# Two-stage expert layer: 17 tiles sorted from the first 24 row tiles run right behind the output projection, 22 tiles after them

## The chip, the cores and the metric

One NeuronCore of a Trainium2 chip runs the whole program. The time is device microseconds of one execution, the median of three; a separate, profiled execution gives the trace. Engines are named as in the profile: PE (TensorE matmul), PEld (its weight loads), DVE (VectorE), ACT (ScalarE), POOL (GpSimd), SP (SyncE, which here only issues transfers).

## The reference

The input x has 4 sequences of 1024 rows of 512 values (4096 rows, 32 row tiles of 128). An RWKV-like layer comes first, then one expert out of eight for each row:

```python
x_prev = x shifted by one row within its sequence
xk, xv, xr = x_prev + (x - x_prev) * tmk, ... * tmv, ... * tmr
k, v, r = xk @ Wk.T + bk, xv @ Wv.T + bv, xr @ Wr.T + br
wkv = scan over time of exponentially weighted averages of v (weights from k)
x1 = layernorm(x + (sigmoid(r) * wkv) @ Wo.T + bo)
probs = softmax(x1 @ wg)                      # 8 experts
e = argmax(probs); gate = probs[e]            # one expert a row
out = layernorm(x1 + gate * (x1 @ W[e].T + b[e]))
```

All is float32. Products that need the accuracy are made as three products of a split operand (`hi` and `lo` parts of float32r: hi*hi, hi*lo, lo*hi).

## The kernel before

**First phase.** The rows are cut into 8 blocks of 512 (`BLOCKS`). `walk` runs a `step` for each block on every engine, with a written-out tail for the last block (`last`; `before` and `earlier` are the two ahead of it). In a block PE makes the projections K, V, R in four chunks of 128 channels (12 matmuls each), DVE runs the scans (`recurrence`, `running_max`, `distance`), POOL makes the `lo` halves (`mix_lo`) and two sums per chunk (`leave`), ACT the exponentials. For a chunk pair ACT gives a reciprocal (`reciprocal_guess`), which waits for DVE's `denominator`, and DVE turns it into the result (`try_guess`, `refine`, `result`, which raises `wkv_done`). The output projection (`project_out`, for the last block `out_last`) waits for `wkv_done`. DVE adds the residual (`add_rows`, `add_last`), ACT normalises (`norm`, `norm_last`), PE turns the rows (`turn_rows`, `turn_last`) and makes the router's logits (`logits`, `logits_last`) after ACT has moved the turned rows (`move_turned`, `move_last`). SP stores the rows x1 to memory.

**Routing.** On DVE, `largest` and `choose` make a one-hot matrix of the chosen expert, PE's `count` multiplies it by a triangular matrix (each row's rank within its expert), and DVE works out each row's place in the sorted list: `split_dest` (to integers and back), `place_slots` and `place_tiles` (one-hot matrices for the place within a tile and for the tile). PE multiplies them (line 609) into the list of row numbers, and DVE writes `ids`. The first 24 row tiles (`EARLY`) are counted before the last 8 (`LATE`), but the list is made once, from all 32. Each chained small operation of DVE goes through `link`, which waits for the end of the one ahead of it.

**Second phase.** 39 tiles (`SORTED` = 32 + 7) of up to 128 rows of one expert each. POOL gathers a tile's rows by `ids` with an indirect transfer, PE turns them (`turn`), ACT copies (`move_gathered`), DVE splits (`split_gathered`), PE makes 12 matmuls (`expert`), DVE adds bias and residual (`add_bias`, `add_gathered`), ACT normalises (`norm2`), POOL scatters to the output. PE turns two tiles ahead. SP loads one bias row for each tile. The experts' weights are split by ACT (`expert_hi`) and then by POOL (`expert_lo`, experts 0 to 4; DVE 5 to 7). POOL splits expert 0 before its last `leave` and the others after `wkv_done` of the last block.

The order of the work is written out by hand on each engine; engines meet only at semaphores:

```python
def link(ins):
    chain[0] += 1
    ins.then_inc(routed, 1)
    dve.wait_ge(routed, chain[0])
...
expert_lo(0)
leave(last, CH - 1)
pool.wait_ge(wkv_done, last * 2 + 2)
for e in range(1, POOL_EXPERTS):
    expert_lo(e)
```

## Time and profile before

| | us |
|---|---|
| median of 3 runs (lowest, highest) | 676.62 (675.92, 677.89) |
| the profiled execution's own time | 679.24 |
| its span in the trace | 677.3 |
| first to last tile of experts on PE | 523.64 to 664.0 |
| PE busy of the span | 591.4 (87%) |
| DVE, ACT, POOL busy | 554.9, 403.9, 307.3 |

The span is what the trace covers; 1.9 us of the profiled execution's own time lie around it. Times of rows count from the span's start. A row that gives "x4" stands for four instructions in a run, and its duration is that of the run. What stands in brackets at a row's end is the idle time of the engine ahead of it and who ended that.

### The profile page before, as it was taken

The page shows a single profiled execution, that of the slowest core. Times are in us where ns is not written, and L with a number is a line of the kernel's source. Part 1 is how long each engine was busy: PE and PEld are TensorE (multiplying, and loading weights), DVE is VectorE, ACT ScalarE, POOL GpSimd, SP SyncE. Part 2 cuts the span into 40 slices and gives each one's busy share as a digit, 9 for nine tenths or more (in the row PEclk, how much of TensorE's full clock was granted, in tenths as well). Part 3 has the DMA queues.
Part 4 walks back from the last instruction along what each step waited for, and adds up shares of the span by engine and source line. Part 5 has one row for each costly group of instructions (what it writes and reads, how often), then busy time and mean ns, then how long its engine had stood idle before and what let it go on. Part 6 is the DMA issues. An engine that isn't in the chain of part 4 may idle for free. (4 is left out here: it accounts for less than half of the span.)

```text
span 677.3 us, 8986 instructions
## 1 busy us (share of the span) xinstructions
PE 591.4 (87%) x2484; PEld 438.7 (65%) x2485; DVE 554.9 (82%) x866; ACT 403.9 (60%) x735; POOL 307.3 (45%) x230
## 2 busy tenths in 40 slices
PE   0576788999999999999999999998665999899992
PEld 0355665676778667668768767855464777676771
DVE  7948899998999999999999899678956566566661
ACT  3346475477567656756757647566331677577773
POOL 4743544443551552463444444248304356465541
PEclk9679899999999999999999999898955899899997
DMA  8030010031022013104104103392204576577650
GB/s 309 3 124 1 0 63 0 2 109 62 16 84 72 32 33 122 31 0 155 31 0 148 41 0 125 137 382 103 59 20 140 147 219 211 184 218 216 213 174 6
DMA packets 36562, 67.60 MB, mean 100 GB/s; under 512 B 8560, under 2 KB 8560, under 8 KB 36532
## 3 DMA queue, kind: packets, MB, share of 16 engines
q1 hardware_dynamic: 30292, 48.29, 21.8%
q0 software_dynamic: 6240, 18.94, 9.0%
q8 instruction: 15, 0.25, 0.2%
q14 instruction: 15, 0.12, 0.1%
HBM read 50.17 MB, written 18.88 MB: 102 GB/s over the span
## 5 line engine op out<-in xcount | busy, mean ns | idle before, releaser
L971 POOL TENSOR_TENSOR mixed<-unsplit,mixed 128x1024 fp32r<-128x1024 f32 x44 | 104.5, 2396 | 133.7 <-ACT mixed L657 133.7
L447 PE MATMUL kb<-mixed,w_kvr 128*128 128x512 f32 x384 | 97.9, 405 | 24.4 <-DVE mixed L1312 16.5
L447 PE MATMUL vb<-mixed,w_kvr 128*128 128x512 f32 x384 | 103.1, 420 | 14.9 <-DVE evn L1150 8.6
L629 PE MATMUL y_ps<-w_e_hi,xgT 128*128 x312 | 110.1, 415 | 3.2 <-issue 1.7
L447 PE MATMUL rb<-mixed,w_kvr 128*128 128x512 f32 x384 | 101.8, 415 | 5.5 <-DVE ee L1164 3.6
L447 PEld LDWEIGHTS kb<-mixed,w_kvr 128*128 128x128 f32 x384 | 73.7, 195 | 43.1 <-issue 16.2
L465 PE MATMUL y_ps<-w_o,rw 128*128 128x512 f32 x224 | 100.7, 592 | 0.0
L447 PEld LDWEIGHTS vb<-mixed,w_kvr 128*128 128x128 f32 x384 | 74.5, 198 | 36.8 <-DVE evn L1150 11.8
L447 PEld LDWEIGHTS rb<-mixed,w_kvr 128*128 128x128 f32 x384 | 73.3, 193 | 27.2 <-issue 6.2
L1101 DVE SCALAR_TENSOR_TENSOR unsplit<-diff,vec,xb 128x512 f32<-128x512 f32 x96 | 74.2, 834 | 7.9 <-PE kb L447 6.0
L981 POOL TENSOR_TENSOR ee<-ee,state 128x512 f32<-128x512 f32 x32 | 35.0, 1093 | 95.6 <-DVE state L1134 94.9
L629 PEld LDWEIGHTS y_ps<-w_e_hi,xgT 128*128 128x128 f32 x312 | 60.5, 194 | 20.1 <-issue 7.1
L465 PEld LDWEIGHTS y_ps<-w_o,rw 128*128 128x128 f32 x224 | 42.5, 190 | 42.5 <-issue 40.7
L1064 POOL DMA_INDIRECT out<-yo,ids x39 | 39.4, 1010 | 60.8 <-ACT yo L951 59.4
L1058 POOL DMA_INDIRECT xg<-x_rows,ids x39 | 44.4, 1138 | 45.0 <-DVE ids L1513 33.5
L672 ACT ACTIVATE e<-state 128x512 f32<-128x512 f32 x32 | 20.2, 631 | 74.7 <-DVE state L1118 74.6
L629 PE MATMUL y_ps<-w_e_lo,xgT 128*128 x156 | 63.0, 404 | 0.0
L657 ACT ACTIVATE mixed<-unsplit 128x1024 fp32r<-128x1024 f32 x48 | 50.5, 1054 | 19.0 <-DVE unsplit L1101 19.0
L1537 DVE SCALAR_TENSOR_TENSOR yo<-y_ps,xg,yo 128x512 f32<-128x512 f32 x39 | 29.3, 751 | 36.9 <-PE y_ps L629 36.9
L1134 DVE TENSOR_TENSOR_SCAN state<-eb,state,e 128x512 f32<-128x512 f32 x32 | 40.8, 1275 | 0.4 <-ACT state L707 0.4
L1111 DVE TENSOR_TENSOR_SCAN state<-kb,state,wdec 128x512 f32<-128x512 f32 x32 | 40.3, 1259 | 0.0
L1141 DVE TENSOR_TENSOR_SCAN state<-eb,state,ev 128x512 f32<-128x512 f32 x32 | 40.3, 1259 | 0.0
(198 smaller groups left out, 1052.4 us busy)
## 6 DMA issues: line engine op xcount, KB each, us to landing
bias<-b_experts SPq DMA_DIRECT2D x39, 256.0 KB, 3.6
w_e_raw<-w_experts SPq DMA_DIRECT2D x8, 1024.0 KB, 11.9
rows<-x SPq DMA_DIRECT2D x28, 256.0 KB, 2.6
x_rows<-rows SPq DMA_DIRECT2D x28, 256.0 KB, 2.1
xb<-xT SPq DMA_DIRECT2D x4, 1026.0 KB, 5.3
xb<-xT SPq DMA_DIRECT2D x3, 1024.0 KB, 5.3
w_raw<-w_square SPq DMA_DIRECT2D x2, 1024.0 KB, 10.1
xb<-xT SPq DMA_DIRECT2D x2, 512.0 KB, 5.0
```

Source lines behind the costliest of these rows:

```text
L447: mm = pe.matmul(bank, w_kvr[m][:, a, h, o:o + P], mixed[m][:, bb, h, :], start=(k == 0), stop=(k == 3 * CH - 1))
L465: mm = pe.matmul(y_ps[:, j % 2, :], rw[:, half, c, j * P:(j + 1) * P], w_o[:, c, :], start=False, stop=(c == CH - 1))
L629: mm = pe.matmul(y_ps[:, parity, :], xgT[:, third, a, c, :], w[:, bass.ds(e, 1), c, :].rearrange("p u o -> p (u o)"), start=(c == 0 and (a ...
L657: act.activation(mixed[m][:, HI, 2 * hp:2 * hp + 2, :], unsplit[m][:, LO, 2 * hp:2 * hp + 2, :], ACT.Copy).then_inc(mixed_hi, 1)
L971: pool.tensor_tensor(mixed[m][:, LO, 2 * hp:2 * hp + 2, :], unsplit[m][:, LO, 2 * hp:2 * hp + 2, :], mixed[m][:, HI, 2 * hp:2 * hp + 2, :] ...
L981: pool.tensor_tensor(ee[:, p, b, :], ee[:, p, b, :], state[:, b, SB, 0:TB], ALU.add).then_inc(den_added, 1)
L1058: pool.indirect_dma_start(out=xg[:, k % RING, :], out_offset=None, in_=x1_rows[:, :], in_offset=bass.IndirectOffsetOnAxis(ap=ids[:, k, :], ...
L1064: pool.indirect_dma_start(out=out_v, out_offset=bass.IndirectOffsetOnAxis(ap=ids[:, k, :], axis=0), in_=yo[:, k % RING, :], in_offset=None ...
L1101: ins = dve.scalar_tensor_tensor(out=unsplit[m][:, LO, h, :], in0=diff[:, h, :], scalar=vec[:, VEC_MK + m, h:h + 1], in1=xb[:, h, 0:TB], o ...
L1111: dve.tensor_tensor_scan(state[:, c % 2, SQ, 1:], kb[:], wdec[:, c:c + 1].to_broadcast([P, TB]), state[:, c % 2, SQ, 0:1], ALU.max, ALU.ad ...
L1134: dve.tensor_tensor_scan(state[:, c % 2, SB, 1:], eb[:], e2[:, c % 2], state[:, c % 2, SB, 0:1], ALU.mult, ALU.add).then_inc(b_scanned, 1)
L1141: dve.tensor_tensor_scan(state[:, c % 2, SA, 1:], eb[:], ev2[:], state[:, c % 2, SA, 0:1], ALU.mult, ALU.add).then_inc(a_scanned, 1)
```

## The change

The list is made twice. From the first 24 row tiles alone the counts give full tiles: with 3072 rows and 8 experts at least `FULL` = 17 tiles are full, whatever the routing, and the first 17 of them, in order of expert, become the first stage. The rows left over and those of the last 8 row tiles fill `MIXED` = 22 tiles, the second stage. The sum stays 39.

- DVE's routing of the first 24 row tiles moves into the last block, between its scans, and grows (which rows are taken, which are left). The logits and turned rows of block `earlier` are moved ahead for it on PE and ACT, and PE's `count` stands between two projections.
- `list_full` (24 small matmuls) makes the first list; then the first stage starts. Its 17 steps are written out, and between them stand the last block's `turn_last`, `logits_last`, its routing on DVE (`choose_late` to `tile_experts`), the second `count` and `list_mixed`.
- POOL splits 6 experts' weights (`POOL_EXPERTS`), and no longer waits for `wkv_done` before expert 1. DVE splits experts 6 and 7. Experts 0 and 1 lie in other memory (`home`), so their loads start when the last input block has been read. ACT copies experts 2 to 6 before the last rows are normalised.
- `place_slots` is one wide `tensor_tensor` for 8 row tiles instead of 8 `tensor_scalar`.
- POOL gathers 6 tiles before the first scatter; ahead of tile 17 it waits for the second list, the last rows and the last gates.

```diff
-POOL_EXPERTS = 5
+POOL_EXPERTS = 6
...
+FULL = -(-(EARLY * P - EXPERTS * (P - 1)) // P)
+MIXED = TILES - FULL + EXPERTS - 1
+SORTED = FULL + MIXED
...
+        def home(e):
+            return (e + EXPERTS - 2) % EXPERTS
```

On PE, the last block:

```diff
+            turn_rows(earlier, 0)
             project(last, V, 1)
...
             project(last, V, 2)
+            logits(earlier, 3, lg_ps[:, earlier * TPB + 3, :])
             project(last, R, 1)
             project(last, K, 3)
+            count(hot_early, EXPERTS * EARLY, 1)
             project(last, V, 3)
```

On PE, behind the projections:

```diff
+            out_last(0)
+            out_last(1)
+            turn_rows(before, 0)
+            out_last(2)
+            logits(before, 0, late_ps[:, 0, :])
+            turn_rows(before, 1)
+            list_full()
+            logits(before, 1, late_ps[:, 1, :])
+            turn_rows(before, 2)
+            out_last(3)
+            logits(before, 2, late_ps[:, 2, :])
+            turn_rows(before, 3)
+            turn(0, 0, 0)
+            logits(before, 3, late_ps[:, 3, :])
+            turn(1, 0, 1)
+            for k in range(FULL):
+                turn(k + 2, (k + 2) // RING, (k + 2) % RING)
+                expert_of_full(k)
...
+                if k == 4:
+                    count(hot_late, EXPERTS * LATE, 2)
+                if k == 10:
+                    list_mixed()
```

On ACT:

```diff
+            expert_hi(2)
+            expert_hi(3)
             deviation(before, 0)
             norm(before, 0)
+            expert_hi(4)
             deviation(before, 1)
             norm(before, 1)
+            move_turned(before, 0)
+            expert_hi(5)
+            expert_hi(6)
+            deviation_last(0)
+            norm_last(0)
+            move_turned(before, 1)
```

On POOL:

```diff
             expert_lo(0)
             leave(last, CH - 1)
-            pool.wait_ge(wkv_done, last * 2 + 2)
             for e in range(1, POOL_EXPERTS):
                 expert_lo(e)
...
+            for k in range(RING):
+                gather(k)
             for k in range(SORTED):
-                if k + AHEAD < SORTED:
+                if RING <= k + AHEAD < SORTED:
+                    if k + AHEAD == FULL:
+                        late_rows()
                     gather(k + AHEAD)
                 scatter(k)
```

On DVE:

```diff
+            def place_slots(part, t, n):
+                shape = [P, n, P]
+                dve.tensor_tensor(part[:], over(slot_q[:, t:t + n, None], shape), over(iota_q[:, None, :], shape),
+                                  ALU.is_equal).then_inc(slot_placed, 1)
...
+            largest(0, EARLY, lg_ps[:, 0:EARLY], lg)
+            choose(0, EARLY, lg, choice, hot_early, 1)
             recurrence(last, 2)
...
+            early_ranks()
             try_guess(last, 0)
...
             cap_gate(last, 3)
+            early_counts_of_tiles()
             denominator(last, 3)
             add_rows(before, 1)
+            early_limits()
+            gates(0, EARLY, gate_e, 1)
             try_guess(last, 1)
             refine(last, 1)
             result(last, 1, 1)
...
+            early_columns()
+            shift(before, 0)
+            split_dest(0, EARLY)
+            shift(before, 1)
+            place_tiles(place_k, 0, EARLY, COLS)
+            for n in range(EARLY // PART):
+                place_slots(place_early[n], n * PART, PART)
+            tile_experts(FULL, taken[:, 1:], iota_row, after_full, expert_full, slot_full)
             add_last(0)
             shift_last(0)
+            dve.wait_ge(listed, 1)
+            dve.tensor_scalar(ids_full[:, :, 0], lists_ps[:, 0:FULL], -1.0, None, ALU.add).then_inc(ids_ready, 1)
...
+            for k in range(FULL):
+                step(k // RING, k % RING)
...
+                if k == 11:
+                    late_ids()
```

Three places of the order, as the compiled programs have it. A row is line, operation, output<-inputs, elements per partition side, and the semaphores it waits for; xN stands for N alike.

DVE, end of the last block, before: from the cap of the last gate (`rb`) to the last `result` (`rw`); `ee` is the denominator and then its product with the guess, `er` the guess, `rows` the residual rows of block `before`.

```order
L1157 TENSOR_SCALAR rb<-rb 128x512 [waits er_ready]
L1164 SCALAR_TENSOR_TENSOR ee<-rb,ee 128x512 [waits den_added,r_capped]
L1194 TENSOR_TENSOR rows<-rows,y_ps 128x512 [waits y_filled,row_loaded1]
L1204 BN_STATS bn<-rows 128x6 [waits y_taken] x2
L1208 BN_AGGR stats<-bn 128x2 [waits bn_done] x2
L1171 TENSOR_TENSOR ee<-ee,er 128x1024 [waits recip_guess]
L1199 SCALAR_TENSOR_TENSOR nmr<-stats,rstd 128x2 [waits rstd_ready]
L1177 SCALAR_TENSOR_TENSOR er<-ee,er 128x1024 [waits guess_tried]
L1187 SCALAR_TENSOR_TENSOR rw<-evn,er 128x1024 [waits num_added,y_filled,newton]
```

The same place now, from the cap to the denominator and what follows it; `counts`, `ranked`, `taken` and `jump` are the early routing's tables by expert:

```order
L1282 TENSOR_SCALAR rb<-rb 128x512 [waits er_ready]
L1558 CAST counts_i<-counts 128x18
L1559 TENSOR_SCALAR counts_i<-counts_i 128x18 [waits routed]
L1560 TENSOR_SCALAR counts_i<-counts_i 128x18 [waits routed]
L1561 CAST whole<-counts_i 128x18 [waits routed]
L1562 SCALAR_TENSOR_TENSOR ranked<-seg_two,whole 128x18 [waits routed]
L1289 SCALAR_TENSOR_TENSOR ee<-rb,ee 128x512 [waits den_added,r_capped,routed]
L1319 TENSOR_TENSOR rows<-rows,y_ps 128x512 [waits y_filled,row_loaded1]
L1566 TENSOR_SCALAR taken<-ranked 128x9
L1567 TENSOR_TENSOR n_taken<-taken 128x8 [waits routed]
L1568 TENSOR_TENSOR jump<-ranked,taken 128x8
L1569 SCALAR_TENSOR_TENSOR jump<-jump,taken 128x8 [waits routed]
```

Five chained table operations stand between the cap and the denominator, which ACT's reciprocal waits for, and four more (with the two gate operations behind these rows) ahead of `try_guess`; the statistics (BN) of `before` have moved behind `result`.

PE, from the second count to the first expert tile, before (`lg_ps` is the list, `xg` a gathered tile):

```order
L588 MATMUL y_ps<-hot_late,behind 128x72 [waits hot_ready,y_taken]
L589 MATMUL y_ps<-hot_late,ones 128x72
L609 MATMUL lg_ps<-place_k,place_q 128x40 [waits tile_placed,slot_placed]
L609 MATMUL lg_ps<-place_k,place_q 128x40 x7
L609 MATMUL lg_ps<-place_k,place_q 128x40 [waits tile_placed,slot_placed]
L609 MATMUL lg_ps<-place_k,place_q 128x40 x7
L609 MATMUL lg_ps<-place_k,place_q 128x40 [waits tile_placed,slot_placed]
L609 MATMUL lg_ps<-place_k,place_q 128x40 x7
L609 MATMUL lg_ps<-place_k,place_q 128x40 [waits tile_placed,slot_placed]
L609 MATMUL lg_ps<-place_k,place_q 128x40 x7
L618 MATMUL t_ps<-ident,xg 128x128 [waits gathered0,tiles_ready]
L618 MATMUL t_ps<-ident,xg 128x128 x3
```

PE now, from the last part of the first list (`lists_ps`) to the turn of the first gathered tile:

```order
L662 MATMUL lists_ps<-place_k,place_early_127 128x32 [waits tile_placed,slot_placed]
L662 MATMUL lists_ps<-place_k,place_early_127 128x32 x7
L546 MATMUL eb<-wgs,x1T 128x8 [waits x1T_moved]
L546 MATMUL eb<-wgs,x1T 128x8 x3
L538 MATMUL t_ps<-ident,rows 128x128 [waits x1_ready]
L538 MATMUL t_ps<-ident,rows 128x128 x3
L517 MATMUL y_ps<-bo_73,ones 128x512 [waits y_taken,wkv_done]
L639 MATMUL y_ps<-w_o,rw 128x512 x4
L546 MATMUL eb<-wgs,x1T 128x8 [waits x1T_moved]
L546 MATMUL eb<-wgs,x1T 128x8 x3
L538 MATMUL t_ps<-ident,rows 128x128 [waits x1_ready]
L538 MATMUL t_ps<-ident,rows 128x128 x3
```

One bank of the output projection (`y_ps<-w_o,rw`), two groups of logits (`eb<-wgs,x1T`) and two turns of rows now stand between the list and the first turn of a gathered tile, in PE's order, and the logits wait for ACT (`x1T_moved`).

DVE now, the two kinds of one-hot matrices and the table of experts (`place_early` for the slots, `place_k` for the tiles):

```order
L1506 TENSOR_TENSOR place_k<-tile_k,iota_k 128x768
L1508 TENSOR_TENSOR place_k<-place_k,token_100 128x768 [waits routed]
L1501 TENSOR_TENSOR place_early_125<-slot_q,iota_q 128x1024
L1501 TENSOR_TENSOR place_early_126<-slot_q,iota_q 128x1024
L1501 TENSOR_TENSOR place_early_127<-slot_q,iota_q 128x1024
L1512 TENSOR_TENSOR after_full<-iota_row,taken 128x136
L1513 TENSOR_REDUCE tile_e<-after_full 128x17 [waits routed]
L1514 TENSOR_SCALAR tile_e<-tile_e 128x17 [waits routed]
L1515 TENSOR_SCALAR moved_e<-tile_e 128x17 [waits routed]
L1516 SCALAR_TENSOR_TENSOR moved_e<-tile_e,moved_e 128x17 [waits routed]
L1518 CAST expert_full<-tile_e 128x17 [waits routed]
L1519 CAST slot_full<-moved_e 128x17 [waits routed]
```

Before, this work was 24 narrow `place_q` operations spread between the last rows' additions, 3 wide `place_k` ones and 4 for the table of experts behind the second count; now it is one unbroken run ahead of `add_last(0)`, and 5 of its operations are 768 or 1024 elements wide.

## Rows read from the trace of the kernel before

**Rows 1.** The page: its header.

```profile
span 677.3 us, 8986 instructions
```

**Rows 2.** Busy time by stage; columns as in the first row.

```profile
core 0: us, PE busy (x) PEld busy (x) DVE busy (x) ACT busy (x) POOL busy (x), PEclk, DMA share, GB/s
...
490.00:499.00 9.00, 8.15 (x40) 8.15 (x40) 2.36 (x2) 3.15 (x7) 0.00 (x0) 0.50 0.08 29
...
505.00:512.30 7.30, 7.17 (x32) 6.97 (x32) 6.24 (x25) 0.00 (x0) 0.00 (x0) 0.50 0.00 0
512.30:520.00 7.70, 0.04 (x1) 0.07 (x2) 4.77 (x4) 0.00 (x0) 6.09 (x4) 0.50 0.58 171
...
523.64:528.80 5.16, 5.16 (x13) 4.00 (x14) 1.54 (x3) 0.60 (x1) 0.00 (x0) 0.52 0.63 150
528.80:664.00 135.20, 128.87 (x601) 100.90 (x599) 87.96 (x225) 98.58 (x226) 73.37 (x70) 0.99 0.63 195
```

**Rows 3.** Timeline of PE: projection bank, logits, list, first gathered tiles, expert tiles (start, duration).

```profile
461.26 3.60 PE L568 MATMUL kb<-w_o,rw 128*128 128x512 f32 x8
464.69 0.95 PE L482 MATMUL eb<-wgs,x1T 128*128 128x8 f32 x8
...
505.04 7.20 PE L609 MATMUL lg_ps<-place_k,place_q 128*128 128x40 f32 x32 [3.60 <-DVE place_k L1423]
519.96 1.08 PE L618 MATMUL t_ps<-ident,xg 128*128 128x128 f32 x4 [7.72 <-DMA xg<-x_rows,ids]
...
523.64 0.79 PE L629 MATMUL y_ps<-w_e_hi,xgT 128*128 x1
...
528.79 0.60 PE L618 MATMUL kb<-ident,xg 128*128 128x128 f32 x4
...
532.01 0.60 PE L618 MATMUL t_ps<-ident,xg 128*128 128x128 f32 x4
```

**Rows 4.** Timeline of DVE: the last block, then the routing up to the list.

```profile
432.20 0.70 DVE L1157 TENSOR_SCALAR rb<-rb 128x512 f32<-128x512 f32 x1 [4.98 <-ACT rb L664]
...
452.14 0.69 DVE L1164 SCALAR_TENSOR_TENSOR ee<-rb,ee 128x512 f32<-128x512 f32 x1 [0.93 <-POOL ee L981]
...
458.04 1.22 DVE L1187 SCALAR_TENSOR_TENSOR rw<-evn,er 128x1024 f32<-128x1024 f32 x1
...
462.88 0.34 DVE L1389 TENSOR_REDUCE mx<-lg_ps 128x24 f32<-128x192 f32 x1
...
504.40 1.29 DVE L1423 TENSOR_TENSOR place_k<-tile_k,iota_k 128x320 fp32r<-128x320 f32 x3
...
512.51 0.20 DVE L1513 SCALAR_TENSOR_TENSOR ids<-lg_ps,empty 128x39 uint32<-128x39 f32 x1
```

**Rows 5.** The same timeline: small operations beside POOL's split, and one without it.

```profile
464.27 1.50 DVE L1395 SCALAR_TENSOR_TENSOR choice<-lg,rank 128x192 f32<-128x192 f32 x1
...
472.24 1.20 DVE L1409 TENSOR_SCALAR dest_i<-dest_i 128x24 int32<-128x24 int32 x1
...
506.91 0.17 DVE L1409 TENSOR_SCALAR dest_i<-dest_i 128x8 int32<-128x8 int32 x1
```

**Rows 6.** Timeline of POOL: the split of experts 1 to 4, the first gather.

```profile
459.35 20.20 POOL L1041 TENSOR_TENSOR w_e_lo<-w_e_raw,w_e_hi 128x512 fp32r<-128x512 f32 x16 [6.09 <-DVE rw L1187]
513.00 2.92 POOL L1058 DMA_INDIRECT xg<-x_rows,ids  x1 [33.45 <-DVE ids L1513]
```

**Rows 7.** Timeline of all engines near the start.

```profile
26.31 5.52 POOL L1034 TENSOR_TENSOR w_kvr<-w_raw,w_kvr 128x2048 fp32r<-128x2048 f32 x1
27.35 7.02 DVE L1101 SCALAR_TENSOR_TENSOR unsplit<-diff,vec,xb 128x512 f32<-128x512 f32 x4
```

**Rows 8.** Timeline of ACT: the copy of one expert.

```profile
458.28 1.90 ACT L852 ACTIVATE w_e_hi<-w_e_raw 128x2048 fp32r<-128x2048 f32 x1
```

**Rows 9.** Timeline of PE: a wait for a gathered tile.

```profile
582.33 0.65 PE L618 MATMUL t_ps<-ident,xg 128*128 128x128 f32 x4 [2.03 <-DMA xg<-x_rows,ids]
```

**Rows 10.** Timeline of all engines at the end.

```profile
663.58 0.40 PE L629 MATMUL y_ps<-w_e_hi,xgT 128*128 x1
```

More of the change, by code:

```diff
@@ L227, in build @@
[L227 to L237 removed]
+        total = place("total", [P, EXPERTS], F32)
@@ L613, in turn, with list_mixed @@
+            def list_mixed():
+                pe.wait_ge(slot_placed, EARLY // PART + 1)
+                pe.wait_ge(tile_placed, 2)
+                for t in range(LATE):
+                    mm = pe.matmul(lists_ps[:, 0:MIXED], place_late[:, t, :], place_k2[:, t, :],
+                                   start=(t == 0), stop=(t == LATE - 1))
+                mm.then_inc(listed, 1)
             def turn(k, r, n):
@@ new lines, in _ @@
+            enter_q(2, *here)
+            move_turned(earlier, 0)
+            norm(earlier, 1)
+            entry_weight(last, 1)
+            move_turned(earlier, 1)
+            decay(last, 1)
+            gate_r(last, 0)
+            weight(last, 1)
+            enter_ab(last, 1, *here)
+            move_turned(earlier, 2)
+            enter_q(3, *here)
+            entry_weight(last, 2)
+            move_turned(earlier, 3)
+            decay(last, 2)
+            weight(last, 2)
+            enter_ab(last, 2, *here)
@@ new lines, in _ @@
+            recurrence(last, 0)
+            shift(earlier, 1)
+            running_max(last, 1)
+            distance(last, 1)
+            try_guess(before, 1)
+            refine(before, 1)
+            result(before, 0, 1)
+            cap_gate(last, 0)
+            denominator(last, 0)
+            recurrence(last, 1)
+            running_max(last, 2)
+            distance(last, 2)
+            dve.wait_ge(mixed_f32, BLOCKS * 6)
+            link(dve.memset(counts[:], 0.0))
+            largest(0, EARLY, lg_ps[:, 0:EARLY], lg)
@@ new lines, in _ @@
+            choose(0, EARLY, lg, choice, hot_early, 1)
+            recurrence(last, 2)
+            cap_gate(last, 1)
+            denominator(last, 1)
+            running_max(last, 3)
+            distance(last, 3)
+            early_ranks()
+            try_guess(last, 0)
+            refine(last, 0)
+            result(last, 1, 0)
+            cap_gate(last, 2)
+            denominator(last, 2)
+            recurrence(last, 3)
+            add_rows(before, 0)
+            cap_gate(last, 3)
@@ new lines, in _ @@
+            early_counts_of_tiles()
+            denominator(last, 3)
+            add_rows(before, 1)
+            early_limits()
+            gates(0, EARLY, gate_e, 1)
+            try_guess(last, 1)
+            refine(last, 1)
+            result(last, 1, 1)
+            add_rows(before, 2)
+            add_rows(before, 3)
+            for j in range(TPB):
+                statistics(before, j)
+            for j in range(TPB):
+                aggregate(before, j)
+            early_columns()
@@ L1483, in _ @@
-            link(dve.tensor_tensor(below[:], over(work_late[:, :, LATE:], [P, EXPERTS, TILES]), steps[:], ALU.is_gt))
-            link(dve.tensor_reduce(ntiles[:], below[:], AX_X, ALU.add))
-            link(dve.tensor_tensor_scan(ends[:], over(one_t[:], [P, EXPERTS]), ntiles[:], 0.0, ALU.mult, ALU.add))
-            link(dve.tensor_tensor(starts[:], ends[:], ntiles[:], ALU.subtract))
-            link(dve.tensor_tensor(work_early[:], over(starts[:, :, None], [P, EXPERTS, EARLY]), hot_e, ALU.mult))
@@ L1497, in _ @@
-            link(dve.tensor_tensor(work_late[:], work_late[:], hot_l, ALU.mult))
-            link(dve.tensor_reduce(dest[:, EARLY:], work_late[:, :, 1:].rearrange("p e t -> p t e"), AX_X, ALU.add))
-            split_dest(EARLY, LATE)
-            place_tiles(EARLY, LATE)
-            place_slots(EARLY, LATE)
-            for j in range(TPB):
-                dve.wait_ge(row_stored[j], last * 16)
-            link(dve.tensor_tensor(after[:], over(iota_k[:, 0:SORTED, None], [P, SORTED, EXPERTS]),
-                                   over(ends[:, None, :], [P, SORTED, EXPERTS]), ALU.is_ge))
@@ new lines, in late_starts @@
+            def late_starts():
+                link(dve.tensor_tensor_scan(ends[:], over(one_t[:], [P, EXPERTS]), n_tiles[:], 0.0, ALU.mult, ALU.add))
+                link(dve.tensor_tensor(starts[:], ends[:], n_tiles[:], ALU.subtract))
+                link(dve.scalar_tensor_tensor(out=first_row[:], in0=starts[:], scalar=float(P), in1=n_left[:],
+                                              op0=ALU.mult, op1=ALU.add))
+                link(dve.tensor_tensor(flat(work_late), flat(work_late), late_counts[0], ALU.add))
```

734 lines of the change are left out of this document (409 added, 325 removed).

## The prediction

> **What bounds the kernel now.** I first read busy time by stage. From 528.8 to 664.0 us PE is busy 128.9 of 135.2 us at the full clock [rows 2], and tiles follow each other after 3.22 us (528.79 to 532.01) [rows 3]: PE's matmuls set the second phase. The first tile, at the lower of the two clock levels (0.52), takes 5.2 us [rows 2]. The last matmul ends at 664.0 [rows 10], 13.3 us ahead of the span's end at 677.3 [rows 1]. Between the phases PE has no such load. The last block's result ends at 459.3 (458.04 + 1.22) [rows 4]; the list's matmuls begin at 505.04 [rows 3], and from 512.3 to 520.0 PE is idle [rows 2]. There the timelines are read next: DVE writes the list of rows at 512.51 [rows 4], POOL starts the first gather at 513.00 [rows 6], PE turns the tile at 519.96, with 7.72 us of idle time put down to that transfer, and the first expert matmul starts at 523.64 [rows 3]. This seam of 64.3 us (459.3 to 523.64) is what the change can shorten: PE needs four banks of 3.6 [rows 3] and small work in it.
>
> So the program now is: seam's end 523.64, plus 140.4 to the last matmul, plus 13.3. All the work of both phases stays; the question is where the first expert matmul lands and what is added behind it.
>
> **DVE beside POOL.** This decides the first term. POOL splits experts 1 to 4 without a gap from 459.35 to 479.55, 16 operations of 1.26 us [rows 6]. In that time an operation of DVE over 24 integers takes 1.20 us; the like over 8 takes 0.17 at 506.91, when POOL is idle [rows 5]. A product of 192 elements with two inputs in SBUF takes 1.50 us beside POOL [rows 5], where a reduction over 192 from PSUM takes 0.34 [rows 4]. Near the start four mixing operations, which have two inputs in SBUF, take 7.02 us together beside an operation of POOL that ends at 31.83 [rows 7]. I read: such an operation of DVE waits for the end of POOL's running one, and chained through `link` each meets the next. I count 1.0 to 1.2 us for each such meeting.
>
> **Part by part: up to the last result.** Added on DVE ahead of `result(last,1,1)`: memset and five operations for the choice, 2.3 us; ranks 1.4; the five table operations behind the cap, of which four meet POOL (now free to split expert 1 there), 4 x 1.2 + 0.3 = 5.1; limits 0.9; gates 0.65. Three of the 1024-wide operations meet POOL's split of experts 0 and 2, 3.7 together. Statistics of 1.9 move away. That is 12.2 us. DVE's idle time in this block is 4.98 at 432.20, which the choice and `recurrence(last, 2)` can now use, and 0.93 at 452.14 [rows 4]; I take 5.5 as hidden. The result ends 6.7 us later, at 466.0. If DVE met POOL nowhere, 4.4 us would remain and be hidden: 459.3.
>
> **From the result to the list.** Two additions, two statistics with their aggregates and a memset took from 459.3 to 462.88 [rows 4]; now it is four statistics and no memset, about 4.8 us, and 0.5 for a late start: 471.3. `early_columns`: five operations with two inputs in SBUF, four of which meet POOL (1.26 each), and 0.6 for the reduction: 476.9. `split_dest`, while POOL waits for ACT, 5 x 0.22: 478.1. Then `shift(before, 1)` waits for ACT, which first normalises two rows and copies expert 4 (1.90) [rows 8]: 481.0. One-hot matrices: 320 elements take 0.43 (three in 1.29), 1024 take 1.22 [rows 4]; so two of 768 at 0.9 and three of 1024 at 1.15 are 5.3 us, and behind each POOL, splitting experts 4 and 5, takes its turn, 5 x 1.1: 491.7. Nine small operations for the tables, 2.0, three of them meeting POOL, 3.5: 497.2. `add_last(0)`, its shift and the list's copy: 2.8, so the list stands at 500.0, not at 512.7. The first list's matmuls (24, where 32 took 7.2) [rows 3] end under the tables.
>
> Without any meeting, columns, matrices and tables are 3.6, 5.4 and 3.5 shorter: 480.8. Both ends are kept.
>
> **To the first expert matmul.** From the list (512.71) to that matmul (523.64) it was 10.9 us [rows 3, 4]: 510.9. But PE has a queue of its own now: `logits(before, 1)` waits until ACT has normalised the last block's first row tile (500.8), and behind it come three groups of logits at 0.95, two turns at 0.6, one bank with its bias row (4.1) and three gathered turns (1.8): 10.0 us at the full clock. PE has little to do ahead of it; before, in such a stretch (490 to 499), the granted clock was 0.50 [rows 2], and I add 2.5 for that. The first expert matmul starts at 513.0, 10.6 earlier. In exchange it runs at the full clock: 5.16 - 3.22 = 1.9 saved.
>
> The Trainium skill says of the clock, in "TensorE: Matmul & The Clock Gate", "What's actually happening", that it is either 1.2 or 2.4 GHz and nothing between; the 0.77 of a mixed stretch is then an average. By it all of this queue could run at the low level, which doubles its 10.0 us in place of my 2.5 more, and the time would be 7.5 us longer, 679.1. The rows do not exclude it: from 490 to 499 PE was busy 8.15 of 9.00 us and stayed at 0.50 [rows 2].
>
> **In the second phase.** PE gets four turns (0.6), four groups of logits (0.95) [rows 3], two counting matmuls (0.6) and eight for the list (0.9, by 7.2 for 32 at half the clock): 7.7, take 7.5. DVE is busy 88.0 of 135.2 us there [rows 2], 2.3 a tile; the late routing is some 45 operations of 0.2 to 0.3, with three wider ones, 13 us over 13 tiles. That makes 3.3 a tile, where PE with its additions has 3.8; no burst is over 1.7 us, and DVE works a tile ahead. I price it at 0 (bounds 0 and 6). `gather(17)` waits for the second list, ready about one tile after `expert(12)`; with 1 us for issue and 4 for landing it arrives before `turn(17)`, ahead of `expert(15)`: 0 (bound 4). A late gather cost PE 2.03 us at 582.33 [rows 9]. Expert 7's split on DVE hides under tiles 0 and 1. The tail, 13.3, is untouched.
>
> **Sum.** 513.0 + (140.4 - 1.9 + 7.5) + 13.3 = 672.3 us of span, 5.0 less than 677.3 [rows 1]. The profiled execution's 679.24 would be 674.2; the median, 2.6 below the profiled time, goes from 676.62 to 671.6.
>
> **Rivals.**
> *POOL hardly collides (faster still).* For it: POOL's splits wait for ACT's copies, so DVE may meet far fewer of them; the order of a few operations decides. With no meeting the list stands at 480.8, PE's queue gives a first matmul near 493.8, and the time is 652.4. Half the meetings give 662. Against it: from 459.35 to 479.55 there was no gap [rows 6]. Chance 0.27 (656 to 667).
> *No change.* The seam is another 3 to 7 us longer: most of PE's queue at the low clock, or the bank `out_last(3)` and the moved rows a step later. 674.6 to 678.6. Chance 0.10.
> *Slower: the late routing stalls the first stage.* POOL issues 70 indirect transfers in the second phase and is busy 73.4 of 135.2 us with them [rows 2]. If casts and integer operations of DVE (16 in the late routing, five in a row in `split_dest`, five in the second table of experts) met those as they meet the split, up to 1 us each, steps 6 and 12 would take 7 us and more, PE would wait 8 to 10 us in all, and `gather(17)` would slip by 3 more: 671.6 + 12 = 683.6. It decides from 7 us of added waits. Against it: POOL there issues transfers and DVE loses little; its tile work fits in 88.0 us. Chance 0.13.
> In "SBUF — State Buffer", "Who interferes with whom", the Trainium skill has casts and `tensor_scalar` in their two-port modes take a port pair shared with GpSimd, whose descriptors for gathers need it too, and whoever comes first blocks the other for the whole instruction. By that rule this rival is likelier than I make it; a run here has not shown it for transfers.
>
> **How the numbers follow.** A measurement of this kernel tells about 0.3% (2 us) from no change. The forecast's case, 671.6 with 667 to 676 as its own range, has 0.50; of it 0.42 lies below 674.6, 0.06 within 0.3% and 0.02 above. With the rivals: faster 0.42 + 0.27 = 0.69, say 0.70; same 0.06 + 0.10, say 0.15; slower 0.02 + 0.13 = 0.15. The range, 656 to 681, leaves out the case without meetings below and the full price of the slow rival above.
>
> **What would show it.** Right: `result` of the last block ending near 466, list near 500, first expert matmul near 513, the last one ending near 659; the four integer operations behind the cap at 1.2 us each; wide one-hot operations at 2 us and more. Wrong: integer operations at 0.2 there; a first expert matmul before 505 or after 518; steps 5 to 12 of the first stage with PE waiting for `turned_lo` or `y_taken`; a PE wait for tile 17's gather over 2 us; tiles of the second stage no longer 3.2 to 3.5 us apart.

## The result, and the profile after

The changed kernel takes 685.17 us (median of 4 runs, 683.71 to 685.70) where the kernel before took 677.25 in the same comparison: a ratio of 1.011, 95% interval 1.0076 to 1.0145. It is slower by 1.1%, and 671.6 was forecast. Its profiled execution has this header, 4.4 us above [rows 1]:

```profile
span 681.7 us, 8970 instructions
```

Busy time by stage of the changed kernel: the wait for the list's matmuls and the tables, PE's queue up to the first expert matmul, the whole second phase (first to last expert matmul), and two single tiles of it. Columns as in the first row.

```profile
core 0: us, PE busy (x) PEld busy (x) DVE busy (x) ACT busy (x) POOL busy (x), PEclk, DMA share, GB/s
...
485.50:498.70 13.20, 5.36 (x24) 5.04 (x24) 12.22 (x20) 2.87 (x5) 9.38 (x6) 0.53 0.00 0
498.70:511.45 12.75, 11.16 (x53) 8.15 (x54) 7.08 (x13) 5.99 (x12) 6.41 (x6) 0.81 0.76 251
...
511.45:668.36 156.91, 142.29 (x670) 112.41 (x670) 101.61 (x276) 102.44 (x236) 73.49 (x70) 0.96 0.59 174
...
531.96:538.41 6.45, 5.24 (x19) 4.08 (x19) 2.65 (x9) 2.76 (x7) 2.58 (x3) 0.74 0.64 205
...
551.73:558.56 6.83, 6.00 (x17) 4.53 (x17) 1.42 (x3) 2.61 (x6) 2.21 (x3) 0.54 0.64 219
```

The first expert matmul now stands at 511.45, where it was at 523.64 [rows 3]: the seam is 12.2 us shorter. But from that matmul to the end of the last one it is 156.9 us, where it was 140.4. The same stretch of before has PE busy 134.0 of 140.4 us, so idle 6.3; now it is busy 142.3 and idle 14.6. So 12.2 us are won, 8.3 lost to PE's busy time and 8.3 to its waits, which makes the 4.4 us between the spans (the tail behind the last matmul is 13.3 us in both).

Timeline of PE in the changed kernel: a group of logits, the first expert matmul, logits of the last block, then turns (L680) and first expert matmuls (L689) that had to wait. The bracket is idle time ahead of the instruction, and what ended it.

```profile
498.76 1.87 PE L546 MATMUL eb<-wgs,x1T 128*128 128x8 f32 x8 [6.43 <-ACT x1T L850]
...
511.45 0.50 PE L689 MATMUL y_ps<-w_e_hi,xgT 128*128 x1 [1.28 <-issue]
...
518.46 1.85 PE L654 MATMUL eb<-wgs,x1T_last 128*128 128x8 f32 x16
...
531.96 0.66 PE L680 MATMUL kb<-ident,xg 128*128 128x128 f32 x4 [2.53 <-DMA xg<-x_rows,ids_full]
533.83 0.52 PE L689 MATMUL y_ps<-w_e_hi,xgT 128*128 x1 [1.22 <-issue]
...
551.73 1.12 PE L680 MATMUL kb<-ident,xg 128*128 128x128 f32 x4 [3.42 <-DMA xg<-x_rows,ids_full]
553.67 0.79 PE L689 MATMUL y_ps<-w_e_hi,xgT 128*128 x1 [0.82 <-issue]
...
590.32 0.65 PE L680 MATMUL t_ps<-ident,xg 128*128 128x128 f32 x4 [1.94 <-DMA xg<-x_rows,ids_mixed]
591.29 0.49 PE L689 MATMUL y_ps<-w_e_hi,xgT 128*128 x1 [0.32 <-issue]
```

Two turns of the first stage wait 2.53 and 3.42 us for a gathered tile, longer than any in the second phase of the kernel before [rows 9], and each wait is followed by a second one of 1.22 and 0.82 us ahead of the next expert tile's first matmul, and by a tile at a lower granted clock (0.74 and 0.54 in the stages above, so roughly half and nearly all of the tile at the lower level, 1.2 GHz of 2.4: 6.45 and 6.83 us in place of 3.2, the second wait included). A third wait, of 1.94 us for tile 19 at 590.32, comes in the second stage, with a granted clock of 0.70 behind it.

The profile names no releaser for the second waits ("issue"). They are not for the new tile's operand, which belongs to an expert step two tiles on: DVE begins its split only at 533.39 and 553.59 and ends it behind the start of those matmuls. What stands there in PE's order are two reads of the tile's tables (its expert and its slot) and the wait for the expert's split weights. In the second stage, and in the kernel before, it is one table read, and the wait there is 0.32 us (591.29 above). Timeline of PE in the kernel before, behind the wait of [rows 9]:

```profile
583.30 0.79 PE L629 MATMUL y_ps<-w_e_hi,xgT 128*128 x1 [0.32 <-issue]
```

That the reads make these waits is likely and not tested. In the whole phase "issue" accounts for 5.2 of PE's 14.6 us of idle time, where it was 1.7 of 6.3 before.

Timeline of POOL in the changed kernel: one split beside DVE's tables, then scatter (L1181) and gather (L1174) ahead of each of the two long waits.

```profile
453.22 4.94 POOL L1157 TENSOR_TENSOR w_e_lo<-w_e_raw,w_e_hi 128x512 fp32r<-128x512 f32 x4
...
525.40 1.03 POOL L1181 DMA_INDIRECT out<-yo,ids_full  x1 [18.77 <-issue]
526.74 0.98 POOL L1174 DMA_INDIRECT xg<-x_rows,ids_full  x1 [0.30 <-issue]
...
543.59 1.02 POOL L1181 DMA_INDIRECT out<-yo,ids_full  x1 [4.79 <-ACT yo L1047]
544.91 1.23 POOL L1174 DMA_INDIRECT xg<-x_rows,ids_full  x1 [0.30 <-issue]
```

The gather of tile 6 goes out at 526.74, behind `scatter(0)`, and lands at 531.96, when PE turns the tile; that of tile 10 goes out at 544.91 behind `scatter(4)` and lands at 551.7. So they take 5.2 and 6.8 us from issue to turn, and the longer landing is part of the second wait. Each time POOL had been idle (18.77 and 4.79 us), standing at a scatter that waits for ACT's normalised rows. Why `scatter(0)` is late is seen on ACT:

```profile
520.84 0.60 ACT L976 ACTIVATE x1T_last<-rb 128x512 f32<-128x512 f32 x1 [4.28 <-PE rb L648]
...
541.93 0.82 ACT L1047 ACTIVATE yo<-yo,nmr,rstd 128x512 f32<-128x512 f32 x1 [0.97 <-DVE nmr L1733]
```

The move of the last block's rows stands ahead of `norm2(0)` in ACT's order and waits 4.28 us for PE. And at 541.93 ACT waits for DVE's `shift2`. Timeline of DVE in the changed kernel: the table operations behind the cap, the last result, early columns, the wide matrices, the list, two splits of gathered tiles (L1710), and a piece of the late routing ahead of that `shift2` (L1733):

```profile
453.32 1.19 DVE L1559 TENSOR_SCALAR counts_i<-counts_i 128x18 int32<-128x18 int32 x1
454.55 1.19 DVE L1560 TENSOR_SCALAR counts_i<-counts_i 128x18 int32<-128x18 int32 x1
...
463.76 2.18 DVE L1312 SCALAR_TENSOR_TENSOR rw<-evn,er 128x1024 f32<-128x1024 f32 x1
...
471.00 1.31 DVE L1575 TENSOR_TENSOR beyond<-beyond,jump 128x192 f32<-128x192 f32 x1
...
480.12 0.83 DVE L1324 SCALAR_TENSOR_TENSOR nmr<-stats,rstd 128x2 f32<-128x2 f32 x1 [2.94 <-ACT rstd L840]
...
483.68 6.71 DVE L1501 TENSOR_TENSOR place_early<-slot_q,iota_q 128x1024 fp32r<-128x1024 f32 x3
...
497.38 0.17 DVE L1643 TENSOR_SCALAR ids_full<-lists_ps 128x17 uint32<-128x17 f32 x1
...
533.39 0.69 DVE L1710 TENSOR_TENSOR xgT<-kb,xgT 128x512 fp32r<-128x512 f32 x1
...
539.33 0.28 DVE L1663 TENSOR_TENSOR_SCAN work_late<-seg_late,lists_ps 128x64 f32<-128x64 f32 x1
...
540.48 0.69 DVE L1710 TENSOR_TENSOR xgT<-t_ps,xgT 128x512 fp32r<-128x512 f32 x1
...
541.74 0.15 DVE L1733 TENSOR_TENSOR nmr<-mean,rstd 128x1 f32<-128x1 f32 x1
```

The late piece of 539.33 holds DVE until 540.44; only then come the next operand's split, a bias addition, and `shift2(4)` at 541.74, for which ACT, POOL's `scatter(4)` and with it `gather(10)` are waiting. ACT's own wait there is 0.97 us, less than a third of the 3.42 that PE then waits.

### The profile page after: what moved, and what is told of

Same layout as the page of the kernel before. It is cut to its first block and busy times, and to the rows that moved or that the text cites. A ratio compares the mean times of both kernels' runs of the same rounds, so it can differ in the third digit from the quotient of the medians.

```text
span 681.7 us, 8970 instructions
## 1 busy us (share of the span) xinstructions
PE 591.1 (87%) x2484; PEld 435.7 (64%) x2485; DVE 565.0 (83%) x873; ACT 403.0 (59%) x735; POOL 319.4 (47%) x237
## 5 line engine op out<-in xcount | busy, mean ns | idle before, releaser
L511 PE MATMUL kb<-mixed,w_kvr 128*128 128x512 f32 x384 | 99.6, 410 | 23.8 <-DVE mixed L1437 16.9
L689 PE MATMUL y_ps<-w_e_hi,xgT 128*128 x312 | 111.0, 418 | 7.3 <-issue 5.2
L689 PEld LDWEIGHTS y_ps<-w_e_hi,xgT 128*128 128x128 f32 x312 | 61.2, 196 | 24.3 <-issue 11.3
L689 PE MATMUL y_ps<-w_e_lo,xgT 128*128 x156 | 63.6, 408 | 0.0
L1157 POOL TENSOR_TENSOR w_e_lo<-w_e_raw,w_e_hi 128x512 fp32r<-128x512 f32 x24 | 38.0, 1614 | 14.1 <-ACT w_e_hi L957 14.1
L1181 POOL DMA_INDIRECT out<-yo,ids_full x17 | 18.1, 1065 | 49.7 <-ACT yo L1047 27.5
L1047 ACT ACTIVATE yo<-yo,nmr,rstd 128x512 f32<-128x512 f32 x39 | 31.8, 816 | 15.2 <-DVE nmr L1733 12.2
```

The costliest lines, as they stand in the source:

```text
L511: mm = pe.matmul(bank, w_kvr[m][:, a, h, o:o + P], mixed[m][:, bb, h, :], start=(k == 0), stop=(k == 3 * CH - 1))
L689: mm = pe.matmul(y_ps[:, n % 2, :], xgT[n % 3][:, a, c, :], w[:, bass.ds(p, 1), c, :].rearrange("p u o -> p (u o)"), start=(c == 0 and (a, ...
L1047: act.activation(yo[n][:], yo[n][:], ACT.Identity, bias=nmr2[:, n:n + 1], scale=rstd2[:, n:n + 1]).then_inc(out_ready, 1)
L1157: part = pool.tensor_tensor(w_e_lo[:, p, c], w_e_raw[:, p, c], w_e_hi[:, p, c].bitcast(F32), ALU.subtract)
```

## The experiments

The first theory is a ring: expert tile k, `norm2(k)` on ACT, `scatter(k)`, then on the same queue of POOL the gather five tiles ahead, its landing, PE's turn. Its slack was small before; the change eats it by late pieces and late rows. Where an expectation numbers theories, the first is this ring; the others leave the ring alone and put the loss in PE's and DVE's own added work, in ACT's order, in ports shared by DVE and POOL, or in a memory so busy that transfers land late. Medians and ratios are of the timed runs, the last four columns of one profiled execution each. A ratio is to the kernel before in the same comparison, whose median was 677.25 for the changed kernel, 677.47 for e1 to e4, 676.74 for e5 to e8 and 675.76 for e9 to e11, so times of different groups differ by up to 1.7 us for that alone:

| Kernel | us, median | ratio to before (95%) | first expert matmul | second phase, us | PE busy | PE idle |
|---|---|---|---|---|---|---|
| before | 677.25 | 1 | 523.64 | 140.4 | 134.0 | 6.3 |
| after | 685.17 | 1.011 (1.0076 to 1.0145) | 511.45 | 156.9 | 142.3 | 14.6 |
| e1 | 671.76 | 0.9886 (0.9833 to 0.9939) | 514.22 | 145.1 | 137.3 | 7.8 |
| e2 | 667.31 | 0.9844 (0.9807 to 0.9882) | 523.12 | 127.9 | 127.3 | 0.6 |
| e3 | 678.23 | 1.0014 (0.9987 to 1.0041) | 512.39 | 149.1 | 138.4 | 10.7 |
| e4 | 681.40 | 1.0061 (1.0028 to 1.0094) | 512.42 | 153.3 | 140.2 | 13.1 |
| e5 | 669.21 | 0.9866 (0.9814 to 0.9917) | 512.81 | 142.4 | 135.5 | 7.0 |
| e6 | 673.74 | 0.9943 (0.9907 to 0.9978) | 512.22 | 148.1 | 139.3 | 8.9 |
| e7 | 665.12 | 0.9805 (0.9756 to 0.9855) | 508.69 | 141.6 | 136.4 | 5.1 |
| e8 | 678.30 | 1.0023 (0.9996 to 1.0050) | 511.23 | 149.1 | 139.3 | 9.8 |
| e9 | 666.30 | 0.9869 (0.9836 to 0.9903) | 520.77 | 127.2 | 127.2 | 0.0 |
| e10 | 664.12 | 0.9823 (0.9788 to 0.9859) | 508.93 | 140.5 | 135.4 | 5.1 |
| e11 | 676.38 | 1.0025 (1.0001 to 1.0049) | 508.26 | 149.6 | 138.2 | 11.4 |

**e1 and e2: the gather ahead of the scatter,** in the changed kernel and in the kernel before. `gather(k + 6)` needs only that DVE has taken tile k out of its slot, not that it is normalised.

```
-AHEAD = 5
+AHEAD = 6
```

e1: 

> The changed kernel with gather(k+6) issued ahead of scatter(k), in place of gather(k+5) behind scatter(k-1). Theory 1: the first stage is bound by a ring of the tiles (expert matmuls, normalisation, scatter, gather, landing, turn), so the late gathers of tiles 6, 10 and 19 and the low clock behind them go: first expert matmul unchanged near 511.5, the stretch from there to the last matmul 146 to 149 us instead of 157, time 675 to 678. Theory 2: PE's own added work and DVE's late pieces make the stretch long and the gathers' waits only take the place of others: time 683 or more. Theory 3: the gathers are late because the memory is busy (landing 6.8 us): they are then issued earlier but land later, time 681 to 685.

e2: 

> The same edit in the kernel before. Theory 1: its second phase had the same ring with less slack used: waits of 2.03 and 0.96 us for gathers and a stretch at low clock behind the first go, 3 to 5 us less, 672 to 674. Theories 2 and 3: no change within 1 us.

Both gained far more than expected: 13.4 us in the changed kernel (685.17 to 671.76) and 10.2 in the kernel before (677.47, its median in that comparison, to 667.31). Timeline of POOL in e1:

```profile
520.72 0.94 POOL L1174 DMA_INDIRECT xg<-x_rows,ids_full  x1 [12.42 <-DVE yo L1726]
529.39 1.02 POOL L1181 DMA_INDIRECT out<-yo,ids_full  x1 [7.73 <-ACT yo L1047]
```

The scatter is even later than in the changed kernel (529.39), but the gather had gone out 8.7 us ahead of it, and PE turns tile 6 without a wait. The ring is shown, and the busy memory is excluded as the main cause, since it would have left the time at 681 or more. e2 says more: in the kernel before, PE's 6.3 us of idle time fall to 0.6 and its busy time from 134.0 to 127.3. So the kernel before already stood at the edge of this ring, and PE's matmuls did not set its second phase alone. But e1 stays 4.5 us slower than e2 although it starts its experts 9 us earlier: the ring is not the whole loss.

**e3: ACT's two moves behind `norm2(0)`.**

```
                 if k == 0:
-                    move_last(2)
-                    move_last(3)
-                norm2(k, k % RING)
+                norm2(k, k % RING)
+                if k == 0:
+                    move_last(2)
+                    move_last(3)
```

> The changed kernel with ACT's copies of the last two turned row tiles behind the normalisation of tile 0, not ahead of it. In the trace ACT waits 4.28 us for PE's turn there, and scatter(0) and gather(6) stand behind. Theory 1: gather(6) is issued 3 to 4 us earlier, PE's wait of 2.53 us and the low clock behind it go: time 681 (3 to 5 less). Theory 2: within 1 us of 685.

It took 6.9 us off the changed kernel: the wait of 2.53 us for tile 6 is gone, and with it the tile at the lower clock. PE's wait for tile 10 is gone too, though DVE's late pieces stand where they stood, so part of that second stall was the first one carried on. The loss at tile 6 was this one order on ACT.

**e4: the late pieces between `shift2(k)` and `add_gathered(k+1)`,** so that `shift2` no longer stands behind them.

```
+                split_gathered(k + 3, (n + 3) % RING)
+                add_bias(k + 2, k // RING + (n + 2) // RING, (n + 2) % RING)
+                shift2(k, n)
+                late_piece(k - 1)
+                add_gathered(k + 1, (n + 1) % RING)
```

> The changed kernel with each piece of DVE's late routing placed between shift2(k) and add_gathered(k+1), where DVE waits for PE, not ahead of the next shift2, which the normalisation, the scatter and the next gather wait for. Theory 1: each tile's normalisation comes up to 1.7 us earlier in steps 1 to 12, tiles 10 to 19 lose their waits (3.4 us, 1.9 us and low clock): time 680 to 682. Theory 2: within 1 us of 685.

Its median is 3.8 us lower, as expected, but its ten runs spread from 678.29 to 686.43 and the intervals of the two ratios overlap, so the size is not settled. The trace shows where it acts: PE turns tile 10 without a wait, where it had waited 3.42 us; the waits that are left are 2.25 us for tile 6 and 1.65 for tile 11. So the late pieces do delay the ring through `shift2`. Since e3 alone takes away the wait for tile 10 as well, the gains of e3 and e4 are not terms to be added.

**e5 and e6: gather first with e3's order (e5), and with e4's too (e6).**

e5: 

> The changed kernel with gather(k+6) issued ahead of scatter(k) and with ACT's two moves of the last block behind norm2(0). If the ring through the scatter's wait was all that stalled the first stage, the moves matter no more once the gather is ahead of the scatter, and this is the time of the gather-first version, 671 to 673 us. If ACT's late norm2(0) also delays the first rows by itself, 667 to 670. First to last expert matmul 143 to 146 us in the one case, 139 to 142 in the other.

e6: 

> The version before with the late routing's pieces of DVE between shift2(k) and add_gathered(k+1), behind split_gathered(k+3), not ahead of it. Theory that DVE's pieces cost PE about half their length in each step once the ring is free (waits of 0.6 to 0.8 us at 6 to 8 tiles): 3 to 5 us less than the version before, and the waits at tiles 6, 10 and 16 gone. Rival that DVE's pieces are hidden and PE's own added work and the transfers are what remains: within 1.5 us of it.

e5 is 2.6 us below e1 (1.4 by the ratios). Its time is in the second of the two outcomes expected and its phase, 142.4 us, between the two, and the intervals of the ratios overlap; the two orders of ACT are not told apart once the gather is first. e6 was a miss: it is 4.5 us slower than e5, where 3 to 5 less were expected. Its cause is not shown, and there are two candidates. With the gather first, what is waited for is `add_gathered`, which frees the slot for the gather and PSUM for PE, and e6 puts the pieces ahead of just that. But the edit also moves each piece one step later (`late_piece(k - 1)`), and the trace shows what follows: POOL waits 7.28 us for the second list ahead of gather(17), where it waited 3.22 in e5, and PE waits 0.64 and 1.07 us at its fixed places for the late count and the late list. No run tells the two apart.

**e7: POOL's splits held back, on e5** ("the first of these" in the expectations of e7 and e8 is e5). Experts 1 to 3 behind the last result, experts 4 and 5 behind the wide matrices.

```
-            for e in range(1, POOL_EXPERTS):
+            pool.wait_ge(wkv_done, last * 2 + 2)
+            for e in range(1, 4):
+                expert_lo(e)
+            pool.wait_ge(slot_placed, EARLY // PART)
+            for e in range(4, POOL_EXPERTS):
                 expert_lo(e)
```

> As the first of these, and POOL starts the splits of experts 1 to 3 only behind the last block's result, and those of experts 4 and 5 only when the three wide one-hot matrices are written. Theory that DVE's operations wait for POOL's running one: the four integer operations behind the cap fall from 1.2 to 0.2 us, the last result ends 3 to 5 us earlier (461 to 463), the one-hot matrices of 1024 take 1.1 us each in place of 2.2, the list stands at 488 to 492 in place of 498, and the time is 3 to 6 us below the first of these. Rival that the list is early enough, since PE's own queue of logits and the bank set the first expert matmul: the operations get shorter, the first expert matmul and the time move by under 1.5 us. If the ports are not the cause, nothing gets shorter.

Timeline of DVE in e7, with the rows that answer to 453.32, 463.76 and 483.68 above:

```profile
454.53 0.18 DVE L1563 TENSOR_SCALAR counts_i<-counts_i 128x18 int32<-128x18 int32 x1
454.74 0.18 DVE L1564 TENSOR_SCALAR counts_i<-counts_i 128x18 int32<-128x18 int32 x1
...
460.91 1.23 DVE L1316 SCALAR_TENSOR_TENSOR rw<-evn,er 128x1024 f32<-128x1024 f32 x1
...
479.78 3.49 DVE L1505 TENSOR_TENSOR place_early<-slot_q,iota_q 128x1024 fp32r<-128x1024 f32 x3
```

The list stands at 494.4 (498.8 in e5), later than the 488 to 492 expected, since the tables behind the matrices now meet POOL's second split (1.18 to 1.30 us for six of them). Table operations behind the cap fall from 1.19 to 0.18 us, the result from 2.18 to 1.23, the three matrices from 6.71 to 3.49. The first expert matmul comes 4.1 us earlier than in e5, and so does the end: 669.21 to 665.12, all four runs below all four of e5, though the intervals of the ratios overlap. The meetings with POOL are shown, by a change of POOL's times alone, and their price is on the path.

**e8: more late work on DVE, on e5.** Five small operations more behind each step of the first stage. The expectation counts 13 steps, but the edit stands in the loop over all `FULL` = 17, and the rows below have 85 more operations of DVE (361 against 276).

```
                 step(k // RING, k % RING)
+                split_dest(0, LATE)
```

> As the first of these, with five more small DVE operations (the split of eight destinations, done again, 0.9 us) behind each of the 13 steps 0 to 12, which doubles what the late routing adds on DVE there. If DVE's work in the first stage is hidden, the same within 1.5 us. If each piece delays the next step's operand by about half its length or more, 5 to 10 us slower.

Busy time of the second phase, e5 and then e8:

```profile
512.81:655.24 142.43, 135.45 (x670) 108.50 (x670) 100.17 (x276) 100.32 (x236) 70.53 (x70) 1.00 0.63 191
```

```profile
511.23:660.31 149.08, 139.31 (x670) 111.86 (x670) 114.72 (x361) 99.88 (x236) 70.10 (x70) 0.97 0.60 183
```

DVE has 14.5 us more to do in the phase. The median is 9.1 us higher, 0.6 for each; in the two profiled executions the phase grows by 6.7, which is 0.46 for each. So DVE's work there was not hidden, although DVE is busy only 100 of 142 us in e5. Its share in one tile is the reason: about 2.5 us of a tile's 3.22 are its own tile work (0.69, 0.74, 0.15, 0.75 and 0.15, in the steps from 540.48 on), so 0.7 are free, and 8 of the 12 late pieces in the changed kernel's trace take 1.0 to 2.0 us in one go. The doubled pieces also end in PE's own queue, timeline of PE in e8:

```profile
558.34 1.88 PE L670 MATMUL lists_ps<-place_k,place_late 128*128 128x22 f32 x8 [2.83 <-DVE place_late L1501]
```

The late list's matmuls stand in PE's order between two tiles and wait there for DVE. So a good part of the 6.7 us is this one wait (2.83), and 0.5 to 0.6 is not a price that each piece pays by itself.

**e9, e10, e11.** e9 repeats e2, e10 repeats e7, and e11 is the changed kernel with e7's holds and nothing else.

e9: 

> The kernel before with gather(k+6) ahead of scatter(k), a second time, to set it beside the best version of the changed kernel on the same chip: 667 us again (666 to 668.5).

e10: 

> The changed kernel with gather(k+6) ahead of scatter(k), the two moves behind norm2(0) and POOL's splits held, a second time: 665 us again (664 to 666.5), so 1.5 to 3 us below the kernel before with the same order of gathers. If the late routing's pieces on DVE and PE's added work gave back the whole of the shorter seam, no difference between the two.

e11: 

> The changed kernel with POOL's splits held and nothing else: gathers and moves as in the changed kernel. If seam and ring are separate terms, as much less than the changed kernel as the holds gave in the other version (4 us): 680 to 682, still slower than before. If an earlier start lets the gathers get further ahead, under 679.

e10 is the fastest of all, 664.12, and beats both kernels by far (0.9823 of the one before). Against the kernel before with the gather first it is 2.2 us ahead, as in the pair of e7 and e2; the intervals of the ratios still overlap, so that the two stages are worth 2 us is possible and not settled. e11 is 8.8 us below the changed kernel, but the two stand in different comparisons: by their ratios (1.0110 and 1.0025) it gained 5.8 us, and these intervals do not overlap. So holding POOL helps here too; that it is worth more than the 4 us of a separate term is not clear of noise. Timeline of PE in e11, the turns that answer to 531.96 and 551.73 of the changed kernel:

```profile
527.66 0.66 PE L680 MATMUL kb<-ident,xg 128*128 128x128 f32 x4 [1.47 <-issue]
...
544.37 0.66 PE L680 MATMUL kb<-ident,xg 128*128 128x128 f32 x4 [1.64 <-DMA xg<-x_rows,ids_full]
```

Busy time by stage of the tiles that follow them:

```profile
527.66:532.31 4.65, 3.69 (x19) 2.97 (x19) 2.74 (x11) 2.76 (x7) 1.82 (x3) 1.00 0.76 246
544.37:549.01 4.64, 3.53 (x16) 2.73 (x17) 1.69 (x5) 2.61 (x6) 2.13 (x3) 1.00 0.98 326
```

Here the waits were 1.47 and 1.64 us, and the granted clock stayed at 1.00. So each long wait of the changed kernel cost its own length and then some 2 us of low clock (PE busy 5.24 and 6.00 us for these tiles there, 3.69 and 3.53 here). Why the two gathers landed in 4.5 and 5.6 us here and in 5.2 and 6.8 there stays open.

## Why the prediction was wrong

**Right, up to the first expert matmul.** The last `result` ends at 465.9 (forecast 466.0), the four operations behind the cap take 1.19 to 1.21 us, early columns 1.26 to 1.31, the matrices 2.2 each. The list stands at 497.4 (500.0) and the first expert matmul at 511.45 (513.0; the prediction's own terms, 500.8, 10.0 and 2.5, add up to 513.3), with the bank and the logits ahead of it and 0.81 of the clock. PE's queue took 12.7 us from its first logits, where 12.5 were forecast, so the case with all of it at the lower level did not come. e7 confirms the reason: without POOL beside them the same operations take 0.18.

**Wrong: "In the second phase".** The step that failed is "DVE is busy 88.0 of 135.2 us there ... no burst is over 1.7 us, and DVE works a tile ahead. I price it at 0". Forecast were 146.0 us from the first to the last expert matmul, measured 156.9. Two things stood behind it. First, the reading of [rows 2] and [rows 3], that PE's matmuls set the phase, took an average for a bound: e2 shows that the kernel before lost 12.5 us of this phase (140.4 to 127.9) to a ring in which the gather stands behind the scatter, and the one wait of 2.03 us that I did read [rows 9] was its sign, not an exception. In the changed kernel ACT's moves (6.9 us by e3) and the late pieces ahead of `shift2` (3.8 by e4, not clear of noise) push that ring over its edge. ACT's two moves have no term in the forecast at all: it put them at nothing without a reason. I had asked what the late routing does to DVE's share, and not what stands behind each piece: `shift2`, ACT's rows, POOL's scatter, the gather. Second, even with the ring out of the way (e5), about half a microsecond is paid for each microsecond of DVE work (e8), because DVE has 0.7 us free in a tile and most pieces are longer (the longest, at 578.77, is 2.0 us in one go, over the 1.7 forecast). What the routing adds on DVE, 10.8 us in the phase (100.17 in e5, 89.33 in e2), comes to an estimated 5 to 7 us at the 0.46 to 0.6 of e8.

PE's busy time is off too. With the gather first in both, PE is busy 135.4 us (e10) and 127.3 (e2), 8.1 more, where 7.5 less 1.9 was forecast. The added groups were sized rightly: in e10 the late turns, logits, counts and list take 7.6 us by their own durations. The 2.5 us on top are not taken apart. Nor did the forecast have a term for PE's waits ahead of a tile's first matmul that the profile puts down to "issue": 3.5 of the 5.1 us that PE is idle in e10, none in e9.

**The rivals.** The slower one had the sign, the size of PE's added waits (8 to 10 us forecast, 8.3 measured) and nearly the sum (683.6), but neither the mechanism nor the place: it forecast long steps 6 and 12, and the waits came for the turns of tiles 6, 10 and 19, in PE's steps 4, 8 and 17. That its number came near is luck. DVE's operations do not meet POOL's transfers as they meet its split. In the changed kernel a cast lies wholly beside a gather, and keeps its 0.18 us; the one behind it takes 0.41 and ends as the transfer does:

```profile
580.16 0.18 DVE L1518 CAST expert_mixed<-tile_e 128x22 int32<-128x22 f32 x1
580.37 0.41 DVE L1519 CAST slot_mixed<-moved_e 128x22 int32<-128x22 f32 x1
```

```profile
579.81 0.98 POOL L1174 DMA_INDIRECT xg<-x_rows,ids_mixed  x1 [0.31 <-issue]
```

and all 38 of the one-element `TENSOR_SCALAR`, one a tile, take 0.153 to 0.156 us, 17 of them wholly beside a transfer. At most 0.23 us is what such a meeting cost in the changed kernel, and 0.3 in e8 (a cast of 0.47 in place of 0.17), where the rival had up to 1. "SBUF — State Buffer", "Who interferes with whom", of the Trainium skill has casts and `tensor_scalar`, in their two-port modes, contend with GpSimd, and the one that issues second blocked for the whole of the other's instruction. For POOL's arithmetic the trace agrees (1.19 us beside it, 0.18 without). For its indirect transfers the cast of 0.18 us wholly inside one does not fit "the whole instruction", and the measurement decides. In which mode an operation ran the trace does not show, so the one-element operations say little about the rule. The rival of few meetings fell, the rival of no change did too.

By seam and phase of the best version against the kernel before in the same order of gathers: set against e2, the experts of e10 start 14.2 us earlier (523.12 to 508.93) and need 12.6 us more (127.9 to 140.5), so 1.6 us of the span are left (664.3 to 662.7). Set against e9, which ran in the same comparison, they start 11.8 us earlier (520.77) and need 13.3 more (127.2), and the span is 1.5 us longer (661.2); but that profiled execution was the fastest of e9's six. So one pair of traces does not even settle the sign, and the 2.2 us rest on the medians. Either way the two stages move work out of a stretch where PE is idle into one where PE, DVE and POOL are all near their limit, and it is paid for there.

## What to carry to other kernels

Before a phase is called bound by its engine, follow one tile round its ring of buffers (compute, store, load into the freed slot, compute) and ask how much slack each link has; where a load stands behind a store in one queue, issue the load first, since that alone was worth 10 us here. Work that is spread over a pipeline is not free below the average busy share: compare each piece with what is free in one step of the engine, and name what stands behind it on that engine. And an engine's idle stretch can be filled by starting its work later as well as earlier: POOL, held back from splitting beside DVE's short chained operations, made the kernel 4 us faster (e7 against e5). Last, set a version against one that ran in the same comparison, and count the operations in its trace: that shows what an edit inside a loop really added.

## What the runs showed of the hardware

Some waits of PE cost more than their length: after 2.53 and 3.42 us, with 1.22 and 0.82 more behind them, the tiles that followed had a granted clock of 0.74 and 0.54 and took 6.45 and 6.83 us. After waits of 1.94 us (changed kernel, 590.32), 2.03 (before, 582.33) and 2.25 (e4, 534.16) it was 0.70, 0.68 and 0.73; after 1.47 and 1.64 us in e11 and 1.65 in e4 it stayed at 1.00. DVE's integer and cast operations of 18 elements take 0.18 us alone and 1.19 beside POOL's split, a 1024-wide product 1.23 and 2.18, a 1024-wide comparison 1.16 and 2.24. POOL's third gather of the first six took 2.32 us where its neighbours took 0.95, in the changed kernel and in e1, e5, e7 and e11 alike; no run here tells why.
